# Storing only the finished sums of a graph aggregation, by a queue that waits on register values

## The reference, cut to what is computed

```python
h = jnp.einsum('nf,hfd->hnd', x, W)
e = jax.nn.leaky_relu(a_s[:, src] + a_d[:, dst], NEG_SLOPE)
m = jax.ops.segment_max(e_h, dst, num_segments=N)
ex = jnp.exp(e_h - m[dst])
den = jax.ops.segment_sum(ex, dst, num_segments=N)
alpha = ex / den[dst]
out = jax.ops.segment_sum(h_h[src] * alpha[:, None], dst, num_segments=N)
...
x = x + gnn(xn) + mix(xn)
x = x + moe(layernorm(x))
```

## Time and profile before

| | us |
|---|---|
| median of 3 runs | 1491.21 (1490.78 to 1492.29) |
| profiled execution, its span | 1489.6 |
| TensorE busy | 1175.3 (79%) |
| VectorE busy | 996.3 (67%) |
| GpSimd busy | 692.2 (46%) |
| ScalarE busy | 499.2 (34%) |
| DMA | 255.70 MB, mean 172 GB/s |

### The profile page before, as it was taken

The page is one execution under the profiler, slowest core; times in us unless marked ns, Lnnn a source line. Parts: engine busy times, 40 slices in busy tenths (PEclk is TensorE's granted clock), DMA queues, the critical chain, the costliest instruction groups (busy, mean ns, idle before and its releaser), DMA issues. The chain is left out here.

```text
span 1489.6 us, 30544 instructions
## 1 busy us (share of the span) xinstructions
PE 1175.3 (79%) x6192; PEld 946.9 (64%) x6193; DVE 996.3 (67%) x2854; ACT 499.2 (34%) x1969; POOL 692.2 (46%) x782
## 2 busy tenths in 40 slices
PE   4996699999999878666672799999991799999900
PEld 4664466666666656444451688888881689999800
DVE  6565388888888867665674588899965234444378
ACT  2453233333333322221121655555521123333301
POOL 1001765666666566666621457676753011111175
PEclk9898599999999998787795799999995799999955
DMA  6062678888888777676757534334413972222155
GB/s 194 30 109 78 142 238 247 238 240 249 249 253 246 234 221 224 207 213 197 222 149 218 195 125 135 127 134 139 143 53 129 343 257 70 70 70 70 61 166 179
DMA packets 219212, 255.70 MB, mean 172 GB/s; under 512 B 57205, under 2 KB 193016, under 8 KB 215640
## 3 DMA queue, kind: packets, MB, share of 16 engines
q1 hardware_dynamic: 177464, 140.79, 30.0%
q0 software_dynamic: 30992, 103.79, 24.1%
q10 hardware_dynamic: 10640, 9.86, 2.1%
HBM read 139.69 MB, written 114.67 MB: 171 GB/s over the span
## 5 line engine op out<-in xcount | busy, mean ns | idle before, releaser
L738 POOL DMA_INDIRECT rows<-node_rows,srcT x391 | 389.0, 995 | 217.5 <-PE pO L1048 107.6
L1048 PE MATMUL pO<-rows,pw 128*128 x1184 | 337.2, 416 | 33.5 <-DVE pw L819 29.4
L835 DVE SCALAR_TENSOR_TENSOR acc<-acc,rsc,pO 128x257 f32<-128x257 f32 x592 | 281.0, 475 | 60.2 <-PE pO L1048 29.9
L1048 PEld LDWEIGHTS pO<-rows,pw 128*128 128x128 f32 x1184 | 216.5, 202 | 78.7 <-issue 51.7
L1408 PE MATMUL pW_<-W_again,aT 128*128 128x256 f32 x800 | 183.1, 383 | 0.4 <-DVE res L1476 0.4
L1408 PEld LDWEIGHTS pW_<-W_again,aT 128*128 128x128 f32 x800 | 149.8, 192 | 19.5 <-DVE res L1476 0.7
L1854 POOL DMA_DIRECT2D ys_rows<-ye x64 | 34.5, 539 | 238.0 <-DVE ye L1805 238.0
L1744 ACT ACTIVATE hT<-pHe,b 128x128 f32<-128x128 f32 x256 | 73.0, 368 | 192.8 <-PE pHe L1770 174.8
L1770 PEld LDWEIGHTS pHe<-xeT,w1e 128*128 128x128 f32 x1024 | 127.4, 196 | 13.7 <-DVE w1e L1795 10.5
L1770 PE MATMUL pHe<-xeT,w1e 128*128 128x128 f32 x1024 | 128.1, 279 | 9.9 <-DVE xeT L1788 9.9
L1779 PE MATMUL pYe<-w,hT 128*128 x512 | 122.1, 382 | 1.2 <-issue 0.6
(11 more groups left out here) (332 smaller groups left out, 1929.1 us busy)
## 6 DMA issues: line engine op xcount, KB each, us to landing
agg_rows<-acc SPq DMA_DIRECT2D x296, 256.0 KB
w<-in_ffn_w SPq DMA_DIRECT2D x32, 512.0 KB, 5.8
xe<-xs_rows ACTq DMA_DIRECT2D x64, 128.0 KB, 2.0
ys_rows<-ye POOLq DMA_DIRECT2D x64, 128.0 KB, 2.0
rows<-node_rows,srcT POOLq DMA_INDIRECT x391
node_rows<-xna SPq DMA_DIRECT2D x25, 136.0 KB, 1.8
xna<-in_x SPq DMA_DIRECT2D x5, 640.0 KB, 11.2
mix_rows<-hx SPq DMA_DIRECT2D x25, 128.0 KB
```

The costliest lines, as they stand in the source:

```text
L738: pool.indirect_dma_start(rows[:, k % RING, :], None, node_rows[:, :], at_row(srcT[:, k:k + 1])).then_inc(s_rows[k % len(s_rows)], 16)
L835: dve.scalar_tensor_tensor(out=acc[:, k % V3, s % HG, 0:D + 1], in0=before, scalar=rsc[:, g % V2, s:s + 1], in1=pO[n % PB][:, 0:D + 1], op ...
L1048: pe.matmul(pO[n % PB][:, 0:D + 1], pw[:, s // HG, s % HG, :], rows[:, ds(at[s % 4], 1), 0:D + 1].rearrange("p c f -> p (c f)"), start=Tru ...
```

## The change

1. A window's sum is stored alone, from the slot of its last step, 128 KB, into `agg_win`, in the order of windows. SyncE does nothing else in that stage: for each of 196 windows it loads the count of steps to wait for and the slot's number (two `value_load`s from `win_tab`), waits on `acced` against that register, and issues the store. Four semaphores are used in turn, at most four stores in flight.
2. The flags, tops and mixed rows that SyncE moved are now issued by ScalarE, and so is `load_tops`.
3. ScalarE frees the halves of `acc`: `free_acc` loads four counts from `half_tab`, waits for the four store semaphores against them, and raises `acc_free`, once for each half. VectorE waits for `acc_free` in place of `s_agg`.
4. In the combine stage SyncE loads the sums plainly, since the windows lie in order; the indirect gather, the copy of row numbers and `last_row` are gone from GpSimd.
5. In setup the two tables `win_tab` and `half_tab` are made by twelve short VectorE instructions and four small matmuls, in place of three and two.

How the windows lie in the 37 groups follows from the inputs: 7 or 8 end in each of the groups 0 to 12, 5 to 7 in groups 13 to 23, 4 or 5 in 24 to 27, and 18 in the last nine together. Chunks that end: 8 or 9 a group early, 13 to 16 in the last full ones.

```diff
+STORES = 4
+ACCS = V3 * HG
-        agg_rows = dram("agg_rows", (GROUPS * G, P, D))
+        agg_win = dram("agg_win", (WINDOWS, P, D))
...
+                    def window_slots():
+
+                        line.do(dve.tensor_scalar(win_tab[:, :, 0], win_i[:, 0, :], 1.0, None, ALU.add))
+                        line.do(dve.tensor_scalar(win_i[:, 1, :], win_i[:, 0, :], 3, None, ALU.arith_shift_right))
...
+                    def half_stores():
...
                             if s % HG == 0 and k >= V3:
-                                dve.wait_ge(s_agg[k % V3], turns_of(k))
+                                wait(dve, acc_free, k - V3)
                                 wait(dve, den_in, k - V3)
...
-                    groups([(1, mean_square), (1, copy_h), (1, fifth), (1, last_flags), (1, last_max), (3, keep_den(0)), (3, keep_den(1)), (1, shrink), (1, exps), (0, copy_eq),
-                            (1, copy_top), (0, copy_on), (0, copy_as)])
+                    def load_flags(g):
+                        wait(act, stat, g - V2, TOP)
+                        act.dma_start(flg[:, g % V2, :], flag_rows[g * G * H:(g + 1) * G * H, :]).then_inc(s_flg[g % V2], 16)
+
+                    @node_tile
+                    def store_x2(t):
+                        wait(act, mixed, t)
+                        act.dma_start(row(mix_rows, t), hx[:, t % 2, :]).then_inc(s_x2[t % 2], 16)
+
+                    def store_top(g):
+                        wait(act, td_in, g)
...
+                    def free_acc(i):
+                        def stage(g):
+                            k = 2 * g + i
+                            if k < 2 * GROUPS - V3:
+                                stored = [act.value_load(half_tab[0:1, k, c:c + 1], min_val=1, max_val=16 * WINDOWS + 1) for c in range(STORES)]
+                                for c in range(STORES):
+                                    act.wait_ge(s_agg[c], stored[c])
+                                act.sem_inc(acc_free.sem, 1)
+                        return stage
+
+                    groups([(2, load_tops), (1, mean_square), (1, copy_h), (1, store_x2), (1, fifth), (0, load_flags), (1, last_flags), (1, last_max), (3, keep_den(0)), (3, free_acc(0)), (3, keep_den(1)), (1, shrink), (1, exps), (0, copy_eq),
+                            (1, copy_top), (1, store_top), (0, copy_on), (3, free_acc(1)), (0, copy_as)])
...
-                    def store(i):
-                        def stage(g):
-                            k = 2 * g + i
-                            for q in range(PARTS):
-                                wait(sp, acced, g, i * HG + (q + 1) * HP)
-                                sp.dma_start(agg_rows[k * HG + q * HP:k * HG + (q + 1) * HP, :, :].rearrange("s p f -> p s f"),
-                                             acc[:, k % V3, q * HP:(q + 1) * HP, 0:D]).then_inc(s_agg[k % V3], 16)
-                        return stage
...
-                    groups([(0, load_flags), (2, load_tops), (1, store_x2), (2, store(0)), (1, store_top), (2, store(1))])
+                    for w in range(WINDOWS):
+                        r, c, turn = WINDOWS - 1 - w, w % STORES, w // STORES
+                        steps = sp.value_load(win_tab[0:1, r, 0:1], min_val=1, max_val=GROUPS * G)
+                        place = sp.value_load(win_tab[0:1, r, 1:2], min_val=0, max_val=ACCS - 1)
+                        sp.wait_ge(acced.sem, steps)
+                        if turn:
+                            sp.wait_ge(s_agg[c], 16 * turn + 1)
+                        sp.dma_start(agg_win[r, :, :], acc_slot[:, ds(place, 1), 0:D].rearrange("p c f -> p (c f)")).then_inc(s_agg[c], 16)
...
+                    def load_sums(t, c, r):
+                        wait(sp, agg_in, t - 2)
...
+                            sp.dma_start(AG[:, c, :, :].rearrange("p h f -> p (h f)"), row(by_node, t)).then_inc(s_AG[c], 16)
...
-                    pipeline(sp, NT, [(0, load_x), (7, store)])
+                    pipeline(sp, NT, [(0, load_sums), (0, load_x), (7, store)], extra=3)
...
-                    def gather(t, c, r):
-                        wait(pool, agg_in, t - 2)
-                        pool.sem_inc(s_gate, 1)
-                        pool.tensor_copy(lr[:, c:c + 1], col(last_row, t)).then_inc(lr_in.sem, 1)
...
-                    pipeline(pool, NT, [(0, gather), (2, with_x), (3, with_bias), (6, with_beta), (8, scatter)])
+                    pipeline(pool, NT, [(2, with_x), (3, with_bias), (6, with_beta), (8, scatter)])
```

More of the change, by code:

```diff
@@ L41 @@
 RING, FLY, LEAD, AHEAD = 40, 4, 48, 2
+STORES = 4
+V2, V3, PB = 2, 3, 4
+ACCS = V3 * HG
 PARTS = 4
@@ L405, in _ @@
                     for j in range(2):
-                        mm = pe.matmul(pE[:, 448:448 + NT], same_win, by_tile[:, j, :], start=(j == 0), stop=(j == 1))
+                        pe.matmul(ended_ps, ones[:, 0:1], ended[:, j, :], start=(j == 0), stop=(j == 1))
+                    for j in range(2):
+                        mm = pe.matmul(ends_of[:, j * P:(j + 1) * P], cnt[:, j:j + 1], ident, start=True, stop=True)
                     mm.then_inc(steps_ps, 1)
@@ L417, in _ @@
                     pe.wait_ge(s_att, 16)
+                    pe.wait_ge(steps_in, 2)
                     for j in range(2 * H):
@@ L688, in build @@
             s_flg, s_top = [sem(f"s_flg{c}") for c in range(V2)], sem("s_top")
-            s_agg = [sem(f"s_agg{c}") for c in range(V3)]
+            s_agg, acc_free = [sem(f"s_agg{c}") for c in range(STORES)], Count(sem("acc_free"))
+            acc_slot = acc[:, :, :, :].rearrange("p v s f -> p (v s) f")
             fetched, as_in = sem("fetched"), Count(sem("as_in"))
@@ new lines, in _, with load_tops @@
+                    tops = top_rows[:, 0:DW * MW].rearrange("n (d c) -> n d c", c=MW)[:, :, 0:H + 1]
+                    def load_tops(g):
+                        if g == GROUPS - 1:
+                            act.wait_ge(s_top, 16 * GROUPS)
+                            for j in range(SJ):
+                                n = min(P, GROUPS * G - j * P)
+                                act.dma_start(ml[0:n, j, :, :], tops[j * P:j * P + n, :, :]).then_inc(s_top, 16)
+                    def free_acc(i):
[7 more added lines that the diff above has]
+                        return stage
@@ L1114, in _ @@
                     sp.dma_start(mbo[:, :], a["mix_b_out"].partition_broadcast(1)).then_inc(consts.sem, 16)
-                    @node_tile
-                    def store_x2(t):
-                        wait(sp, mixed, t)
-                        sp.dma_start(row(mix_rows, t), hx[:, t % 2, :]).then_inc(s_x2[t % 2], 16)
                     sp.wait_ge(s_gad, 16 * SJ)
@@ L1138, in store_top @@
-                    def store_top(g):
-                        wait(sp, td_in, g)
-                        by_half = top_rows.rearrange("(t s) w -> t (s w)", s=HG)[2 * g:2 * g + 2, 0:P * MW]
-                        sp.dma_start(by_half.rearrange("i (p c) -> p i c", c=MW), topd[:, g % V2, :, :]).then_inc(s_top, 16)
-                    tops = top_rows[:, 0:DW * MW].rearrange("n (d c) -> n d c", c=MW)[:, :, 0:H + 1]
-                    def load_tops(g):
-                        if g == GROUPS - 1:
-                            sp.wait_ge(s_top, 16 * GROUPS)
-                            for j in range(SJ):
-                                n = min(P, GROUPS * G - j * P)
-                                sp.dma_start(ml[0:n, j, :, :], tops[j * P:j * P + n, :, :]).then_inc(s_top, 16)
@@ L1150, in _ @@
-                    groups([(0, load_flags), (2, load_tops), (1, store_x2), (2, store(0)), (1, store_top), (2, store(1))])
+                    for c in range(STORES):
+                        sp.sem_inc(s_agg[c], 1)
+                    for w in range(WINDOWS):
[6 more added lines that the diff above has]
+                        sp.dma_start(agg_win[r, :, :], acc_slot[:, ds(place, 1), 0:D].rearrange("p c f -> p (c f)")).then_inc(s_agg[c], 16)
@@ L1155, in _ @@
                     sp.dma_start(md_rows.rearrange("(j p d) m -> p j (d m)", p=P, d=DW), mdT.rearrange("p j d i h -> p j (d i h)")).then_inc(moves.sem, 16)
-                    for c in range(V3):
-                        sp.wait_ge(s_agg[c], PARTS * 16 * len(range(c, 2 * GROUPS, V3)))
+                    for c in range(STORES):
+                        sp.wait_ge(s_agg[c], 16 * len(range(c, WINDOWS, STORES)) + 1)
                     moves.wait(sp)
```

61 lines of the change are left out of this document (34 added, 27 removed).

## The result

The changed kernel takes 1579.9 us (1576.8 to 1585.0), the kernel before 1491.2 us beside it: a ratio of 1.060, 95% interval 1.058 to 1.062. Slower, by 89 us, in a range forecast as 1520 to 1600 and 21 us above the value forecast. The profiled execution has a span of 1575.1 us, 85.5 more than before.

A forecast was written before the change was run, and what follows sets the result against it. TensorE bounds early groups and combine, late groups wait for gathers; ScalarE's topd-to-asb path has 0.3 us slack. Early 57 + 1, late -4, clock 8, stage end 2, combine 2, setup 1.5: 67.5 us, hence 1559 us; range 1520 to 1600.

The forecast's parts named there:

- the early sum: ScalarE between topd and asb: asb 2.95 us later, 2.7 per group after slack; with zlow's delay 2.85, +57 us.
- Store of the tops: ScalarE between topd and onT: waiting for topd and issuing the store starts onT 0.53 us later.
- Loads and waits: ScalarE ahead of asb: four table loads at 0.55 us each, 2.2 us, plus 0.2 us for four waits and the release.
- the rival of slow loads: Table loads take 0.5 to 0.6 us each, 1 us more in 32 groups: 1595 us, chance 0.12.
- The mixed rows' store: ScalarE, in front of zlow: a 0.33 us store that, with the wait for its copy, sticks out 0.15 us.
- The clock: TensorE at half clock behind the new stops, 1.7 us a group; a quarter of 0 to 34 us taken, +8 us.
- The late groups: Aggregation's last 14 groups: ScalarE's delay against fewer gather waits, 259 us plus 4 for late gathers against 267: -4 us.
- The combine stage: SyncE's plain loads stand behind weights and x2 rows, first tile some 4 us later: +2 us, 0 to +6.
- the end of the stage: End of aggregation: the five loads of the tops go in front of ScalarE's last releases, +2 us.
- faster case: Late groups lose gather waits, topd-to-asb path grows under 0.3 us early and 1.3 late: about 1467 us, chance 0.07.
- The rival of the clock: TensorE's clock falls behind nearly every stop: +34 us instead of +8, 1582 us, chance 0.14.
- The slots' release: Rival: releases so early that nothing is delayed, or SyncE stores as late as before: near 1491 us, chance 0.03.

The follow-up runs named there:

- The loads moved away: Changed kernel with the second half's free_acc moved from ahead of copy_as to behind the second denominator copy, all loads and waits kept: 1486.9 us, ratio 0.997.
- the kernel with all edits and four more: Four unused single table loads ahead of the asb copies, added to the kernel with all edits: 1547.8 us, ratio 1.038.
- The kernel before with four loads: Kernel before the change, plus four single table loads with unused values on ScalarE directly ahead of copy_as: 1626.5 us, ratio 1.090.
- The filled kernel: Changed kernel with eight more transposes on TensorE ahead of each group's score matmuls, into a bank part nobody reads: 1568.9 us, ratio 1.053.
- the edit that took the wait away: Changed kernel with the combine stage's first two loads of sums issued ahead of the weights and residual rows: 1569.2 us, ratio 1.052.
- the kernel with all edits: Changed kernel with second free_acc moved earlier, one load for four counts, tops' store behind copy_as, first two sums loaded ahead of weights: 1464.3 us, ratio 0.983.

## Why the prediction was right, and where it was off

**The engine and the place: right.** The forecast rested on 0.3 us of slack between asb and the score matmul, and on 2.95 us put ahead of it. It expected TensorE to lose 0.3 us of that at the output projection and to stop for 2.4 us ahead of the scores. The stop is there, 2.96 us on average, all in one place (from 200 to 500 us TensorE waited for onT 5 times, 0.8 us in all); that it equals the 2.95 us of the sum is chance, since 3.36 us were put in. The loads moved away give back 93 us. It was 18.64 us a group against 17.72 expected and 0.4 for the clock.

**The terms of the early sum.** Store of the tops: 0.53 us expected; onT starts 0.74 us behind topd in place of 0.22, so 0.52. Loads and waits: 2.4 expected, 2.84 measured (4.63 less 1.79). Of it the four loads took 2.65 us against 2.2, from 433.40 to 436.05, since one of them took 0.67 us; four undisturbed ones, in the kernel with all edits and four more, take 2.16 (429.80 to 431.96). The price of a load was right. That a load can be slower was the rival of slow loads: 0.45 us more for the four here, where it had 1 us. The mixed rows' store (0.15 us expected) cost nothing: zlow starts 1.10 us behind asb's end, and 1.18 us before. An early group at full clock takes 18.1 us, 0.4 above the sum.

**The clock.** 8 us expected, a quarter of the stops followed by half clock. By the first node-sum matmuls it is 9 of 20 (2.3 to 2.8 us in place of 1.47), and groups so slowed take 19.4 against 18.1 us, 1.3 us each: 12 us. More groups than taken, each at less than the 1.7 us taken.

**The late groups: the term that failed in its result.** -4 us expected, +1.2 measured. The 4 us that the sum adds for late gathers were not needed: asb waits 0 us for them. The kernel before with four loads shows that longer groups alone can do that. Against it, the first two groups took 37.0 us, where two at 17.7 were expected, and the other twelve 19.26 us each, where the sum has 18.65: 2 and 7 us more. What was too small is the stop: 1.8 us in the sum, 2.4 on average over the last eleven groups (1.8 to 3.4). The clock is not what the sum left out, for its base of 16.85 us was itself a period at half clock for much of its length, as its stretch and the first node-sum matmuls in it show (1.47 us at full clock):

```profile
566.55:583.39 16.84, 13.90 (x56) 10.23 (x55) 12.38 (x32) 4.33 (x26) 11.60 (x12) 0.80 0.77 230
```

```profile
567.83 2.77 PE L1048 MATMUL pO<-rows,pw 128*128 x6
```

The filled kernel's 259.2 us for the 14 groups equal the sum's 259 by chance; it has another clock (0.87) and other stops. Why the stop is 0.6 us longer than the sum had it, I have not taken apart.

**The combine stage: a term too small.** +2 us expected for it and +2 for the end of the stage; +13.7 measured. The prediction saw that the sums stand behind the weights on SyncE and put it at 4 us, taking the third tile's row for the measure. The first sums were waited for 16.4 us. By the edit that took the wait away, it was worth 12.9 us of the profile (737.3 less 724.5), and 11 us of the kernel's time.

**The rivals.** Its faster case was that the path from topd to asb must grow by under 0.3 us: late groups at 237 us, 1467 us in all. With the loads moved the late groups took 234.9 us, so that part was priced well; the changed kernel lacks its condition. That the kernel with all edits takes 1464.3 us is a nearness by chance: its early groups are 11 us longer than before, where that case has nothing, its late ones 35 us shorter instead of 30, and its combine stage gained by an edit of its own. The rival of the clock should read 1585 us by its own terms (26 more than 1559), not 1582. Slow loads (1595 us) hold in part, where large stores are near, which this change had just taken away. The slots' release was not too late, and SyncE's own loads, two to each window (here those of the steps), held nobody: no wait in `free_acc` was real.

```profile
L1181 SPq TENSOR_LOAD <-win_tab x196: 262/271/511, 152.5 to 831.0; - x196
```

In sum: 7 us less for setup and what lies around, 10 us more early, 5 more late, 10 more behind group 36 than forecast, together the 18 us that the span is above 1557. The time lies in the range because the largest term, the loads on ScalarE's path, was right; the smaller ones were nearly all too low.

## What to carry to other kernels

An engine that is busy a third of its time may still have no room at one place of its period: read the slack from one period, start to start, and ask for each new queue instruction between which two waits it stands. Register loads are work, 0.54 us each with their checks; load several values at once, and put them behind a wait that ends late anyway. An issue that is moved from one side of an instruction to the other can stay on the path, as the tops' store did. A change can bring its gain on one resource (here 32 us in the late groups, once the loads are out of the way) and lose three times that on a queue, and then the fix is one line in the order, not the change undone.

## What I had not expected of the hardware

- A table load is not a fixed price. One of sixteen values took 1.02 us with no large store beside it, 1.43 us with 256 KB stores spread over the period, 1.61 us with stores leaving beside it, and 2.56 us (up to 3.09) right behind the issue of a burst of four, all medians; a single value 0.28 us alone and 0.54 us among stores.
- Several values in one load are cheap: four values 0.32 us, one value 0.28 us (medians from 200 to 498 us), though sixteen take 1.02.
- The same four loads cost 84 us in one kernel and 136 us in another. In the first the block of loads grew by 2.3 us and 12 of the 20 early groups were at half clock behind the stop, in the second by 4.2 us and all 20.
